# Feed-forward weight operands made inside the feed-forward groups instead of during attention

## The reference

```
xn  = layernorm(x)
att = softmax(causal(q k^T / sqrt(512))) v @ o_proj + xn      # q, k, v from layernorm(xn)*gamma+beta
h   = silu(xn @ w_gate) * (xn @ w_up)                         # 2048 x 2048 hidden
h   = keep the 2 largest |h| of each 4 neighbours, zero the rest
out = x + att + h @ w_down
```

## Time and profile before

| | |
|---|---|
| median of 3 executions | 891.43 us (889.54 to 897.34) |
| the profiled execution, its own time | 898.84 us |
| its span, first to last instruction | 897.0 us |
| mean granted TensorE clock | 0.958 of full |
| PE / PEld busy | 823.1 / 675.6 us |
| DVE busy | 574.0 us |
| ACT / POOL busy | 308.5 / 88.1 us |
| DMA | 167.39 MB, mean 187 GB/s |

### The profile page before, as it was taken

The page is one execution under the profiler, slowest core; times in us unless marked ns, Lnnn a source line. Parts: engine busy times, 40 slices in busy tenths (PEclk is TensorE's granted clock), DMA queues, the critical chain, the costliest instruction groups (busy, mean ns, idle before and its releaser), DMA issues. The chain is left out here.

```text
span 897.0 us, 9757 instructions
## 1 busy us (share of the span) xinstructions
PE 823.1 (92%) x3635; PEld 675.6 (75%) x3635; DVE 574.0 (64%) x975; ACT 308.5 (34%) x504; POOL 88.1 (10%) x163
## 2 busy tenths in 40 slices
PE   7985974899969978979999999999999999999997
PEld 5774863788758867757888888888788888888875
DVE  6985574464552444546386658669966686668696
ACT  5423315322141333324334233425433243324341
POOL 3144322330000440000000000000000000000000
PEclk9997996989989988998999999999999999999999
DMA  9444793757021559975851642446347715442202
GB/s 319 162 153 153 250 326 126 249 199 292 24 71 36 207 218 354 321 305 234 314 227 82 258 164 83 176 188 251 133 156 263 296 58 203 164 164 95 94 0 94
DMA packets 49599, 167.39 MB, mean 187 GB/s; under 512 B 5088, under 2 KB 5136, under 8 KB 47120
## 3 DMA queue, kind: packets, MB, share of 16 engines
q1 hardware_dynamic: 39600, 146.56, 43.7%
q10 hardware_dynamic: 9952, 20.21, 6.5%
HBM read 116.40 MB, written 50.36 MB: 186 GB/s over the span
## 5 line engine op out<-in xcount | busy, mean ns | idle before, releaser
L648 PE MATMUL bank<-X_hi,wset 128*128 128x512 f32 x448 | 175.8, 392 | 7.9 <-DVE X_lo L944 7.0
L649 PE MATMUL bank<-X_lo,wset 128*128 128x512 f32 x448 | 175.4, 391 | 0.0
L650 PE MATMUL bank<-X_hi,wset 128*128 128x512 f32 x448 | 175.3, 391 | 0.0
L648 PEld LDWEIGHTS bank<-X_hi,wset 128*128 128x128 f32 x448 | 84.8, 189 | 26.8 <-issue 9.1
L650 PEld LDWEIGHTS bank<-X_hi,wset 128*128 128x128 f32 x448 | 84.8, 189 | 17.7
L649 PEld LDWEIGHTS bank<-X_lo,wset 128*128 128x128 f32 x448 | 84.8, 189 | 17.5
L1111 DVE TENSOR_TENSOR acc<-bank,acc 128x512 f32<-128x512 f32 x64 | 43.5, 689 | 75.6 <-PE bank L726 75.2
L724 PE MATMUL bank<-dw,hs_hi 128*128 128x512 f32 x224 | 87.2, 390 | 0.0
L726 PE MATMUL bank<-dw,hs_lo 128*128 128x512 f32 x224 | 87.2, 389 | 0.0
L725 PE MATMUL bank<-dw,hs_hi 128*128 128x512 f32 x224 | 87.2, 389 | 0.0
L524 PE MATMUL bank<-v_hi,pT_hi 128*128 128x512 f32 x136 | 59.7, 439 | 20.6 <-DVE pT_lo L930 20.6
(11 more groups left out here) (161 smaller groups left out, 1465.4 us busy)
## 6 DMA issues: line engine op xcount, KB each, us to landing
wset<-w_operands SPq DMA_DIRECT2D x64, 896.0 KB, 8.0
w_operands<-u_hi SPq DMA_DIRECT2D x32, 448.0 KB, 2.9
w_operands<-u_lo SPq DMA_DIRECT2D x32, 448.0 KB, 4.3
dw<-down_operands SPq DMA_DIRECT2D x14, 1024.0 KB, 6.9
u_raw<-w_units SPq DMA_DIRECT2D x32, 256.0 KB, 3.8
xn_t<-xt_raw ACTq DMA_DIRECT2D x8, 512.0 KB, 4.9
d_raw<-L_ffn_w_down SPq DMA_DIRECT2D x8, 512.0 KB, 6.6
down_operands<-d_hi SPq DMA_DIRECT2D x8, 512.0 KB, 5.3
```

The lines of the kernel that those rows point to most:

```text
L648: pe.matmul(dst[:], u[:, 0, :], x_hi, start=(first and kt == 0), stop=False, skip_group_check=True)
L649: pe.matmul(dst[:], u[:, 0, :], x_lo, start=False, stop=False, skip_group_check=True)
L650: last = pe.matmul(dst[:], u[:, 1, :], x_hi, start=False, stop=(kt == 1), skip_group_check=True)
```

## The change

The weight units and their stores are gone from attention, and so are `paced`, `RUNS` and the two DRAM tensors. In each feed-forward group n, the operands for group n+1 are now made in place: SP loads the raw blocks (`load_set`), POOL makes the sums for two blocks at a time (`sums`, 256 elements per partition), ACT the high parts (`operands_hi`, 896 elements) and POOL the low parts (`operands_lo`, 896 elements). w_down comes raw too: ACT `down_hi`, POOL `down_lo`, 1024 elements each, two per two groups. Both passes over the rows make them again. Set 0 is made in the tiles 13 and 14 of attention. The scaling `xn` moves from DVE to POOL, the transfers xw, row_store, row_spread, xt_load and xn_store move from ACT's queue to SP's, the fronts of chunks 1 to 3 have other places, and the first sums for the feed-forward input stand before the last tile's attend.

```diff
-              11: [*z[3], *v[3], ("RUN", 1, 0)]}
-    beside = {0: [xh_pre[1][0], exp[1], v[0][3], xh_pre[1][1]],
-              1: [exp[2], *xh[1], *stat[3], x_stats[3], x_rstd[3]],
-              2: [exp[3], x_scale[2], row_turn[2], row_store[2]],
-              3: [v[1][2], exp[4], *xn[1], xt_load[2], xn_store[1], row_spread[2]],
-              4: [v[1][3], exp[5], *xh_pre[2]],
...
+    between = {3: [z[1][1], row_turn[2], row_store[2], *z[1][2:4], row_spread[2]],
+               7: z[2],
+               11: z[3]}
+    beside = {0: [v[0][1], *stat[2][2:4], x_stats[2], x_rstd[2], xt_load[2]],
+              1: [xh_pre[1][0], v[0][2], xh_pre[1][1]],
+              2: [*xh[1], v[0][3], x_scale[2], xn_store[0]],
+              3: [*xn[1], stat[3][0], stat[3][1]],
...
+              5: [v[1][1], *xh_pre[2], x_scale[3], xn_store[1]],
+              6: [v[1][2], row_turn[3], row_store[3], *xh[2], row_spread[3]],
...
+            def load_set(q):
+                for m in range(4):
+                    sp.dma_start(sums_at(q, m)[:, 0:4, :], w_units[4 * (q % NQ) + m]).then_inc(w_raw_loaded[q % 2][m], 16)
...
+            def sums(q, h):
+                s1, s2, s3, s4, a11, a12, a22 = (pair_at(q, h, o) for o in (S1, S2, S3, S4, A11, A12, A22))
...
+                nc.gpsimd.tensor_tensor(s1, s3, a22, ALU.add).then_inc(w_step, 1)
...
+                nc.gpsimd.tensor_tensor(s4, a12, s2, ALU.subtract).then_inc(w_summed, 1)
+            def operands_lo(q, m):
+                pool.wait_ge(w_hi, 4 * q + m + 1)
+                nc.gpsimd.tensor_tensor(wset[q % 2][:, m, 1, :, :], sums_at(q, m), wset[q % 2][:, m, 0, :, :].bitcast(F32),
+                                        ALU.subtract).then_inc(w_op_ready, 1)
...
+            for q in range(1, N_Q):
+                sums(q, 0)
+                sums(q, 1)
+                operands_lo(q, 0)
+                operands_lo(q, 1)
+                if q % 2 == 1 and q >= 3:
+                    down_lo((q - 3) // 2)
+                operands_lo(q, 2)
+                operands_lo(q, 3)
+            down_lo(ND // 2 - 1)
...
-                pe.wait_ge(wset_loaded[n % 2], 64 * (n // 2 + 1))
                 X_wait(0)
+                pe.wait_ge(w_op_ready, 4 * n + 2)
...
+                pe.wait_ge(w_op_ready, 4 * n + 4)
                 block_product(1, n, A11, B11, X[1], True)
...
                 nc.scalar.activation(g_sum[0][:], g_sum[0][:], ACT.Silu).then_inc(silu_ready, 1)
+                down_next = n >= 2 and n % 2 == 0
+                if n + 1 < N_Q:
+                    operands_hi(n + 1, 0)
+                    operands_hi(n + 1, 1)
                 snapshot(0, n, F_P6, bank[0], g_sum[1], 4 * (n - 1) + 4 if n else 0, 0)
                 snapshot(1, n, F_P6, bank[1], a_tile(n, 1), 0, 0)
+                if down_next:
+                    down_hi(n // 2 - 1)
+                elif n + 1 < N_Q:
+                    operands_hi(n + 1, 2)
+                    operands_hi(n + 1, 3)
...
+                if down_next:
+                    operands_hi(n + 1, 2)
+                    operands_hi(n + 1, 3)
```

More of the change, by code:

```diff
@@ L74, in attention_ffn @@
[L74 to L77, removed]
-               11: [*z[3], *v[3], ("RUN", 1, 0)]}
-    beside = {0: [xh_pre[1][0], exp[1], v[0][3], xh_pre[1][1]],
-              1: [exp[2], *xh[1], *stat[3], x_stats[3], x_rstd[3]],
-              2: [exp[3], x_scale[2], row_turn[2], row_store[2]],
-              3: [v[1][2], exp[4], *xn[1], xt_load[2], xn_store[1], row_spread[2]],
-              4: [v[1][3], exp[5], *xh_pre[2]],
[L84 to L90, removed]
+    steps += [*stat[0], x_stats[0], x_rstd[0], qk[0], qk[1], split[2][0], split[3][0], qk[2], split[2][1], split[3][1], qk[3],
+              xw_load[2], xt_load[1], split[2][2], split[3][2], split[2][3], split[3][3], x_scale[0], ("x_rows", 0, 0), vo[0], vo[1],
+              ("x_turn", 0, 0), *xh_pre[0], vo[2], xh[0][0], stat[1][0], xh[0][1], stat[1][1], vo[3], xh[0][2], stat[1][2], xh[0][3],
+              stat[1][3], x_stats[1], x_rstd[1], *xn[0], xw_load[3], *z[0][0:2], x_scale[1], z[0][2], row_turn[1], row_store[1], z[0][3],
+              ("scores", 0, 0), row_spread[1], exp[0], v[0][0], *stat[2][0:2]]
@@ L97, in attention_ffn @@
             steps.append(("scores", i + 1, 0))
-            if ("exp", i + 1, 0) not in beside.get(i, []) and i < 8:
-                steps.append(("exp", i + 1, 0))
+            if i < 8:
+                steps.append(exp[i + 1])
         steps += [*beside.get(i, []), ("attend", i, 0)]
@@ L105, in key_tiles @@
         return [range(g, min(g + TC, i + 1)) for g in range(0, i + 1, TC)]
[L110 to L144, removed]
     HEAD = 2
@@ L196, in attention_ffn @@
         first_raw = at("first_raw", 144 * KB, [P, 2, G * W], F32)
-        xw = at("xw", 80 * KB, [P, TC, D], F32)
+        xw = [at(f"xw{i}", o * KB, [P, TC, D], F32) for i, o in enumerate((80, 120))]
         rows_wide = at("rows_wide", 88 * KB, [P, 4, TC, P], F32)
[L199 to L206, removed]
+        spread = [at("spread0", 48 * KB, [P, 2, W], F32)] + [at(f"spread{c}", o * KB, [P, 4, W], F32) for c, o in ((1, 24), (2, 56), (3, 88))]
         X_hi = [at(f"X_hi{o}", 8 * o * KB, [P, 2, W], F32R) for o in range(NOP)]
@@ L432, in _ @@
-            for s in range(RINGS):
-                sp.wait_ge(unit_stored[s], 32 * uses[s])
-            load_set(0)
+                    load_set(0)
+            sp.wait_ge(prod_full, len(prod_no))
+            for c in (0, 1):
+                sp.wait_ge(xn_stored[c], 32)
+            load_X(0, B11, 0, 0)
+            load_X(0, T3, 0, 1)
+            load_X(0, B22, 2, 1)
+            load_X(0, B21, 2, 0)
+            load_set(1)
             sp.wait_ge(rows_ready, NT)
@@ L784, in _ @@
                     act.wait_ge(xh_affine, affines)
-                    if n in (1, 2) and k == 0:
-                        act.wait_ge(xn_stored[n - 1], 32)
+                    if n == 2 and k == 0:
+                        act.wait_ge(xn_stored[1], 32)
+                    if n == 3 and k == 0:
+                        act.wait_ge(xn_ready[1], 2)
                     nc.scalar.copy(xT_hi[n][:, k, :], h).then_inc(xh_hi_ready, 1)
+                elif kind == "x_turn":
+                    act.wait_ge(rows_turned, 4)
+                    for row in range(2):
+                        nc.scalar.copy(spread[0][:, row, :], row_bank[row][:]).then_inc(rows_kept, 1)
                 elif kind in ("qk_weight", "vo_weight", "z", "v"):
@@ L833, in _ @@
                     if n == NT - 1:
-                        X_loads()
+                        X_halves(0, range(4))
                 elif kind == "attend":
@@ L1010, in _ @@
                     nc.vector.tensor_tensor(part, part, row_over(n, 3), ALU.add).then_inc(xh_scaled, 1)
-                elif kind == "xn":
-                    if n == 0:
-                        dve.wait_ge(rows_turned, 4)
-                    t = xt_raw[n][k]
-                    done = step(nc.vector.tensor_tensor(t[:], t[:], row_over(n, 0), ALU.mult))
-                    dve.wait_ge(vec_step, done)
-                    nc.vector.tensor_tensor(t[:], t[:], row_over(n, 1), ALU.add).then_inc(xn_ready, 1)
                 elif kind == "row_turn":
```

286 lines of the change are left out of this document (129 added, 157 removed).

## The result

| | before | changed |
|---|---|---|
| median | 892.2 us (889.54 to 897.34, 4 runs) | 965.12 us (963.14 to 966.3, 4 runs) |
| profiled execution | 898.84 us | 965.22 us |
| its span, mean granted clock | 897.0 us, 0.958 | 963.4 us, 0.940 |

The changed kernel is slower by 8.1%: ratio 1.081, 95% interval 1.076 to 1.086. The forecast was 933, range 846 to 958: the sign was right, the size was not.

A forecast was written before the change was run, and what follows sets the result against it. PE was taken to bound the feed-forward part, so gains lay in attention. Terms 61 + 29 + 5 + 2 - 55 = +42 gave 941 us against the profiled 898.84, or 933 us against the median; range 846 to 958.

The forecast's parts named there:

- Attention, forecast -55: Attention: less idle time and less clock loss save 55 us, between -30 and -70.
- Idle time: forecast -40: Attention: of PE's 59.5 us of waits, 19 kept or new, so 40 us of idle time gained.
- kept and new: Attention's remaining PE waits: chunk 1's front 6, pT_lo 1.5, after z 4.5, last tile 4, POOL's xn 3; together 19 us.
- Clock: forecast -15: Attention: low clock cost PE 20 us; with long stalls gone, three quarters of it, 15 us, comes back.
- The stalls in the groups, forecast 61 + 2: Groups 2 to 14: POOL delays DVE's add, PE waits 4.4 or 5.0 each, 61 us; groups 1, 7, 8 add 2.
- the line I drew: POOL's price per low part, extended from 128 and 512 elements: 2.14 us for 896, 2.42 for 1024.
- rival 1: Before the add of F_P7: bf16 counts and keeps not excluded, or POOL loses at each boundary; 846 us, chance 0.25.
- The clock in the groups, forecast 29: Feed-forward groups: each stall is followed by half clock, 2.2 us in each of 13 groups, 29 us.
- Rival 2: Feed-forward groups: the stalls come but the clock does not drop; 904 us, chance 0.15.
- The tail, forecast 5: Last stretch: POOL's last two low parts of w_down and ACT's two casts fall into its first chain, 5 us.
- Rival 3: Feed-forward groups: POOL becomes the bound, PE waits 2 to 3 us more a group; 965 us, chance 0.08.
- rival 4: Whole kernel: half the stalls, about 30 with 12 of clock, nearly cancel -50 in attention; 888 us, chance 0.10.

The follow-up runs named there:

- dose experiment: The changed kernel with POOL's low parts of a set's blocks cut from 896 to 16 and to 512 elements: 888.03 us and 921.18 us.
- 861 us kernel: Changed kernel with v products earlier, turn later, low parts on DVE (placed anew for groups 0, 1, 8), chunk 1's xn late: 861.05 us, 0.964 of before.

## Why the prediction was wrong

The sum was +42, 941 against a profiled 898.84. Measured was 965.22, 24 more. Term by term:

- **Attention, forecast -55, measured -30.6. This is the step that failed**, in both its halves.
  - *Idle time: forecast -40, measured -25.0.* The failed step is the list "kept and new", which came to 19 and has nothing for a placement that stands in the diff: v directly ahead of its attend, eight gaps of 14.3 us in all. I had seen that z loses its cover when v goes from between it and the scores, but did not ask where v went and who waits for it. Chunk 1's front is the second miss: booked at 6 and 3, it costs 5.1 at the turn inside z[0] and 8.0 at z[1], with 1.7 of exclusion in it. The others were near: four gaps after z, 6.3 for 4.5, and the last tile 3.2 for 4. The two edits that undo the placements took 15.5 us of idle time out.
  - *Clock: forecast -15, measured -8.* What attention had lost was sized nearly right; the failed step is how much of it would come back. The trace of before grants half clock in eight stretches of attention. The first row is the longest, then the sum of all eight, then that of the four stretches in the changed kernel:

```profile
130.70:151.20 20.50, 4.27 (x11) 3.40 (x12) 11.52 (x27) 10.03 (x15) 8.85 (x16) 0.50 0.51 171
sum 66.00, PE 33.24 PEld 26.12 DVE 31.63 ACT 32.36 POOL 23.37; mean PE 4.16 PEld 3.27 DVE 3.95 ACT 4.04 POOL 2.92
sum 23.90, PE 17.05 PEld 13.26 DVE 13.34 ACT 5.96 POOL 9.01; mean PE 4.26 PEld 3.32 DVE 3.33 ACT 1.49 POOL 2.25
```

  PE worked for 33.2 of these 66 us, so it lost half of that, 16.6, where I had 20 from 40. In the changed kernel it works for 17.1 at half clock and still loses 8.5. These four stretches lie at the new stalls: at the turn, at the gap behind z[0] that follows it, at chunk 1's front, and in the last tile. "Three quarters" had left too little for them. Busy time fell by 5.6 and not by 8.1; the listed ends at more gaps are about 1 of that, and the rest stays open.
- **The stalls in the groups, forecast 61 + 2, measured 62.0 of idle time.** Right in mechanism and size: 4.25 and 4.78 for 4.4 and 5.0, and the dose experiment gave the formula at three widths. Group 2 was 7.2: there the eight sums stood beside the counts too, before the low parts. POOL's price was above the line I drew: 2.37 mean for 2.14, 2.68 for 2.42. But these means hold POOL's own waiting for DVE; beside PSUM reads an 896 took 2.2. The exclusion does hold for the bf16 counts (0.42 became 2.5), and for the keeps where POOL reached them, in group 2 (a pair took 3.31 for 1.29). POOL wins each boundary, and rival 1 was false. The Trainium skill, "SBUF — State Buffer", section "SBUF: two separate sides", has the lock held for a whole instruction; the trace agrees for these types too.
- **The clock in the groups, forecast 29, measured 32.9 of busy time.** PE works at half clock for 68.3 us there, for 5.8 before, which is 31 lost. Rival 2, stalls without a clock drop, was false.
- **The tail, forecast 5, measured 2.2.**
- **Rival 3** gave 965, the time that was measured, by a mechanism that was not there: PE never waited for wset or for sums, and groups 2 to 14 stall as in the forecast case. Two small slips stand in the rivals: the terms of rival 4 come to 890 with the tail and not 888, and the 3 in rival 1's sum has no term behind it. Neither touches the forecast.
- **From profiled time to median.** I took 7.4 off. The profiled execution of before stood at the upper end of that kernel's executions: in 17 others the clock runs from 0.958 (897.97 and 899.22 us) to 0.965 (890.57). The changed kernel's stood at its own median, so nothing came off there. That is the other 8 of the 32 us between 933 and 965. Taking the profiled minus the median of before over to the changed kernel was a second, smaller error. Without it the range's upper end would have been 965, where the result lies.

The text said that if attention gained under 30 us, chunk 1's front or SP's queue would be the cause. It gained 30.6. No wait that the trace of attention lists is for one of the row transfers in SP's queue; chunk 1's front was a part of it (4.1 us over its 9), and the largest part was the order of PE's own queue, v directly ahead of its attend.

## What to carry to other kernels

Before work is given to POOL beside a dense DVE, add up POOL's holds that fall ahead of the instruction someone waits for: DVE loses their sum. Splitting the work does not help; another moment, where DVE reads PSUM, or DVE itself, does. When a diff lays queues out anew, look up for each moved producer its first consumer and what stands between them: with nothing between, a cast and a subtraction (1.6 us here) are paid at each place. And before a clock loss is booked as a gain, add up the time that PE works, not idles, at half clock. Half of that is lost, and it comes back only where no new stall takes the place of the old ones.

## What the runs showed of the hardware that was not expected

- A DVE instruction that takes one of its operands from PSUM is left alone, and leaves POOL alone: `add_down` took 0.69 beside POOL's low parts, and these took 2.2 each (8.83 for four), against 2.5 to 2.7 in the contended stretch.
- Stalls of 0.9 to 1.7 us in the groups brought no half clock anywhere. Those of 2.2 to 3.8 did in some places and not in others (one of 2.2 in group 2 of the 861 us kernel did, those of 3.0 and 3.3 in its group 8 did not, four of five at 3.15 did). Those of 4 and more did each time in the groups, but one of 4.35 in attention of the same kernel, at 145.58, did not.
- PE worked for half of the half-clock time in attention before (33.2 of 66), and for three quarters of it in the changed groups (68.3 of 88.7), so the mean granted clock alone does not give the loss.
- Execution times of one and the same kernel moved with the granted clock: before, 0.007 of clock (0.965 and 0.958) went with 7 to 9 us.
